# Routed rows of a mixture-of-experts layer: gathered through an index table built on chip, in place of a scatter into a slot buffer

## The reference

```python
def _L0_ffn_ref(x, router_w, w_fc, w_proj, shared_fc, shared_proj):
    TOP_K = 2
    flat = x.reshape(T, D)
    probs = softmax(flat @ router_w.T)               # 8 experts
    topk_p, topk_i = jax.lax.top_k(probs, TOP_K)
    topk_w = topk_p / jnp.maximum(topk_p.sum(-1, keepdims=True), 1e-09)
    combine = jnp.zeros((T, E)).at[jnp.arange(T)[:, None], topk_i].add(topk_w)
    for e in range(E):
        out = out + _mlp(flat, w_fc[e], w_proj[e]) * combine[:, e:e + 1]
    return out + _mlp(flat, shared_fc, shared_proj)  # _mlp: square(relu(x @ fc.T)) @ proj.T

x = x + 0.5 * _L0_ffn_ref(_layernorm(x), ...)
x = x + _L0_attn_ref(_layernorm(x), ...)             # a small MLP trained over 1024 steps, then applied
x = x + 0.5 * _L0_ffn_ref(_layernorm(x), ...)
```

## Time and profile before

| what | us |
|---|---|
| median of 3 runs | 660.36 (660.12 to 660.38) |
| profiled execution | 662.61, of which its span is 660.9 |
| MoE layer 0: tiles, first square to last matmul | 40.1 to 195.3 |
| middle layer, up to the second MoE layer's norm | 213 to 461 |
| MoE layer 1: tiles, first square to last matmul | 486.0 to 640.7 |

### The profile page before, as it was taken

The page is one execution under the profiler, slowest core; times in us unless marked ns, Lnnn a source line. Parts: engine busy times, 40 slices in busy tenths (PEclk is TensorE's granted clock), DMA queues, the critical chain, the costliest instruction groups (busy, mean ns, idle before and its releaser), DMA issues.

```text
span 660.9 us, 11626 instructions
## 1 busy us (share of the span) xinstructions
PE 499.5 (76%) x3496; PEld 445.3 (67%) x3496; DVE 331.5 (50%) x1204; ACT 297.8 (45%) x769; POOL 246.3 (37%) x365
## 2 busy tenths in 40 slices
PE   0673269999980789999999999955671279999970
PEld 0562169999970479999999999832561179989970
DVE  4751045344335557777777777726650035434423
ACT  3321035777760245555455455432420045767750
POOL 2047700444450123545445455430047600444440
PEclk9987569999995699999999999978566579999995
DMA  9921106000009500000000000000001160001007
GB/s 277 239 44 49 52 0 160 28 28 28 32 19 219 66 1 1 1 1 2 1 1 2 1 1 2 0 1 1 0 28 53 49 158 1 27 28 34 28 18 190
DMA packets 41146, 31.01 MB, mean 47 GB/s; under 512 B 3806, under 2 KB 36709, under 8 KB 41088
## 3 DMA queue, kind: packets, MB, share of 16 engines
q1 hardware_dynamic: 36544, 21.80, 14.3%
q0 software_dynamic: 4544, 8.47, 3.9%
HBM read 15.55 MB, written 15.61 MB: 47 GB/s over the span
## 4 chain that ended last, share of the span: by engine, by line
PE 65%; another core or an unknown queue 11%; DVE 10%; ACT 4%; DMA 3%; issue 3%; POOL 2%; SPq 1%; DVEq 0%; ACTq 0%; POOLq 0%
PE bank L916 18%; PE bank L567 14%; PE bank L557 7%; PE bank L550 4%; PE bank L548 4%; PE bank L549 4%; PE bank L504 2%; DMA stage<-y_dram 2%; PE bank L816 2%; DVE stats L379 1%; PE bank L837 1%; PE bank L818 1%; ACT sq L861 1%; PE bank L531 1%
## 5 line engine op out<-in xcount | busy, mean ns | idle before, releaser
L1029 POOL DMA_INDIRECT y_dram<-y_out,stage x78 | 75.8, 972 | 157.6 <-ACT y_out L646 145.6
L1236 DVE TENSOR_TENSOR sq<-bank,relu 128x512 f32<-128x512 f32 x110 | 75.9, 691 | 115.4 <-ACT relu L632 56.1
L567 PE MATMUL bank<-proj_w,hid_t 128*128 (+1 forms) x880 | 123.2, 286 | 11.0 <-issue 10.8
L567 PEld LDWEIGHTS bank<-proj_w,hid_t 128*128 128x128 f32 x880 | 113.3, 201 | 12.5 <-issue 12.5
L632 ACT ACTIVATE relu<-bank 128x512 f32<-128x512 f32 x110 | 65.8, 598 | 119.9 <-PE bank L550 60.8
L557 PE MATMUL bank<-ident,sq 128*128 128x128 f32 x440 | 70.4, 285 | 55.5 <-DVE sq L1236 41.8
L557 PEld LDWEIGHTS bank<-ident,sq 128*128 128x128 f32 x440 | 56.9, 147 | 75.1 <-DVE sq L1236 46.1
L1023 POOL DMA_INDIRECT slots_dram<-rows,slots x64 | 63.3, 989 | 99.6 <-issue 53.1
L638 ACT COPY hid_t<-bank 128x512 f32<-128x512 f32 x110 | 63.9, 581 | 27.2 <-remote 13.9
L911 POOL TENSOR_TENSOR sq<-sq,last_rows 128x128 f32<-128x128 f32 x48 | 22.0, 458 | 86.3 <-DVE sq L892 86.3
L1241 DVE SCALAR_TENSOR_TENSOR res<-bank,res 128x128 f32<-128x128 f32 x32 | 9.3, 291 | 66.5 <-remote 59.6
(11 more groups left out here) (238 smaller groups left out, 1285.1 us busy)
## 6 DMA issues: line engine op xcount, KB each, us to landing
slots_dram<-pad SPq DMA_DIRECT2D x2, 2535.0 KB, 20.2
stage<-slots_dram SPq DMA_DIRECT2D x18, 260.0 KB, 5.6
stage<-y_dram SPq DMA_DIRECT2D x16, 256.0 KB, 5.0
stage<-experts SPq DMA_DIRECT2D x3, 768.0 KB, 8.4
proj_w<-experts SPq DMA_DIRECT2D x1, 2304.0 KB, 15.9
y_dram<-y_out,stage POOLq DMA_INDIRECT x78
res<-x SPq DMA_DIRECT2D x2, 512.0 KB, 5.8
slots_dram<-rows,slots POOLq DMA_INDIRECT x64
```

The costliest lines, as they stand in the source:

```text
L567: last = nc.tensor.matmul(bank[4 + i % 2][:, 0:P], hid_t[:, i % 2, f_cols], proj_w[:, k, f_cols], start=j == 0, stop=j == FJ - 1)
L1029: nc.gpsimd.indirect_dma_start(y_dram.ap(), bass.IndirectOffsetOnAxis(tiles[:, t, P:P + 1].bitcast(U32), 0), y_out[:, t % YBUFS, :], None, ...
L1236: nc.vector.tensor_tensor(sq[:, i % 2, :], bank[i % 2][:], relu[:, i % 2, :], ALU.mult)\
```

## The change

- The scatter, the DRAM slot buffer, its fill and its reload are gone, and so are ACT's copy of `ln` and the 130-wide rows (`ln` is a tile of its own). SP stores `ln` to `ln_dram` once per layer.
- After L455 `route` splits each slot number into tile and row and makes `tile_id`: for each of the 32 (choice, block) columns, 40 numbers that hold the token's id + 1 in the column of its tile, else 0. VectorE makes `row_hot`, a 128-wide one-hot of the row, in four parts, one ahead of each of the turns 0 to 3 (`make_hot`). TensorE adds 32 products of the two in bank 7, eight behind each of the turns 1 to 4 (`table`): a 128 x 40 table with the id + 1 of the pair in each slot. In turn 5 VectorE turns it into two index lists, `to_row` and `from_row` (`make_index`).
- POOL then gathers each tile's 128 rows of 128 numbers from `ln_dram` by one indirect DMA: 20 tiles at once (GATHERED), then one more ahead of each of the waits for `y_made` of tiles 0 to 18. The y scatters stay, 39 per layer, with `to_row` as index.
- The limits of the index check lie in two registers set once.
- `y_out` has 8 buffers. ACT only copies into it; the weight is applied in `add_routed`, by one `scalar_tensor_tensor` for each block and choice (32 of 128 columns a layer, where there were 8 adds of 512).

```diff
-YBUFS = 4
+YBUFS = 8
...
             dve_link(dve, nc.vector.tensor_reduce(slot_f[:], where[:].rearrange("p k b e -> p (k b) e"), AX.X,
                                                   ALU.add), at)
-            nc.vector.tensor_copy(slots[:], slot_f[:]).then_inc(slots_done, 1)
+            dve_link(dve, nc.vector.tensor_copy(slots[:], slot_f[:]), at)
+            nc.vector.tensor_scalar(slot_row[:], slots[:], P - 1, None, ALU.bitwise_and)
+            dve_link(dve, nc.vector.tensor_scalar(slot_tile[:], slots[:], 7, None, ALU.logical_shift_right), at)
+            hot = [P, NSLOT, NCOL]
+            dve_link(dve, nc.vector.tensor_tensor(tile_id[:], iota_t[:].unsqueeze(1).to_broadcast(hot),
+                                                  slot_tile[:].unsqueeze(2).to_broadcast(hot), ALU.is_equal), at)
+            nc.vector.tensor_tensor(tile_id[:], tile_id[:].bitcast(F32), ids[:].unsqueeze(2).to_broadcast(hot),
+                                    ALU.mult)
...
+        def make_hot(c):
+            n = NSLOT // HOT
+            hot = [P, n, P]
+            c = slice(c * n, (c + 1) * n)
+            nc.vector.tensor_tensor(row_hot[:, c, :], iota_p[:].unsqueeze(1).to_broadcast(hot),
+                                    slot_row[:, c].unsqueeze(2).to_broadcast(hot), ALU.is_equal).then_inc(hot_done, 1)
+        def make_index(dve, at, f):
+            dve.wait_ge(table_done, f + 1)
+            table = bank[7][:, 0:NT]
+            dve_link(dve, nc.vector.tensor_scalar(empty[:], table, 0.0, float(NO_ROW), ALU.is_equal, ALU.mult), at)
+            dve_link(dve, nc.vector.scalar_tensor_tensor(to_row[:], table, -1.0, empty[:], ALU.add, ALU.add), at)
+            nc.vector.tensor_scalar(from_row[:], to_row[:], T - 1, None, ALU.bitwise_and).then_inc(index_done, 1)
...
+            def table(c):
+                pe.wait_ge(hot_done, f * HOT + c + 1)
+                for n in range(c * NSLOT // HOT, (c + 1) * NSLOT // HOT):
+                    last = nc.tensor.matmul(bank[7][:, 0:NCOL], row_hot[:, n, :], tile_id[:, n, :], start=n == 0,
+                                            stop=n == NSLOT - 1)
+                if c == HOT - 1:
+                    last.then_inc(table_done, 1)
...
-                nc.scalar.mul(y_out[:, t % YBUFS, :], bank[4 + i % 2][:, 0:P], tiles[:, t, P + 1:P + 2])\
-                  .then_inc(y_made, 1)
+                nc.scalar.copy(y_out[:, t % YBUFS, :], bank[4 + i % 2][:, 0:P]).then_inc(y_made, 1)
...
             def pool_tiles(f):
-                for b in range(NBLK):
-                    for k in range(TOPK):
-                        n = k * NBLK + b
-                        nc.gpsimd.indirect_dma_start(slots_dram[f].ap(),
-                                                     bass.IndirectOffsetOnAxis(slots[:, n:n + 1], 0),
-                                                     rows[:, k, b, :], None, bounds_check=NT * P - 1,
-                                                     oob_is_err=False).then_inc(scattered, 16)
+                def gather(t):
+                    if f == 0 and t == NT - 3:
+                        pool.wait_ge(w_lo_done, E + 1)
+                    nc.gpsimd.indirect_dma_start(tile_rows(t), None, ln_dram.ap(),
+                                                 bass.IndirectOffsetOnAxis(from_row[:, t:t + 1], 0),
+                                                 bounds_check=from_limit, oob_is_err=False)\
+                      .then_inc(tiles_in[t // GRP], 16)
+                pool.wait_ge(index_done, f + 1)
+                pool.wait_ge(ln_stored, 16 * (f + 1))
+                for t in range(GATHERED):
+                    gather(t)
                 for t in range(NT):
+                    if t + GATHERED < NT:
+                        gather(t + GATHERED)
                     pool.wait_ge(y_made, f * NTILES + NS + t + 1)
-                                                 bass.IndirectOffsetOnAxis(tiles[:, t, P:P + 1].bitcast(U32), 0),
-                                                 y_out[:, t % YBUFS, :], None, bounds_check=TOPK * T - 1,
+                    nc.gpsimd.indirect_dma_start(y_dram.ap(), bass.IndirectOffsetOnAxis(to_row[:, t:t + 1], 0),
+                                                 y_out[:, t % YBUFS, :], None, bounds_check=to_limit,
                                                  oob_is_err=False).then_inc(y_stored[t % YBUFS], 16)
...
                 for i in range(NTILES + 2):
+                    if i < HOT:
+                        make_hot(i)
+                    elif i == HOT + 1:
+                        make_index(dve, at, f)
                     if i < NTILES:
                         squared(i)
...
+                        for b in range(g * GRP, (g + 1) * GRP):
+                            last = nc.vector.scalar_tensor_tensor(
+                                res[:, b, :], y_rows[:, k, b * P:(b + 1) * P], weight[:, k, b:b + 1], res[:, b, :],
+                                ALU.mult, ALU.add)
```

More of the change, by code:

```diff
@@ L31 @@
 NTILES = NS + NT
+NCOL = NT + NT % 2
 NQ = (NT + GRP - 1) // GRP
-ROW = P + 2
-PAD_ROW = 1 << 20
+NSLOT = TOPK * NBLK
+NO_ROW = 1 << 13
+HOT = 4
+GATHERED = 20
 PER_WORD = 8
 NWORDS = (NT + PER_WORD - 1) // PER_WORD
-YBUFS = 4
+YBUFS = 8
 NLOADS = 3
@@ L143, in mk_macaron @@
         res = sb("res", [P, NBLK, P])
-        rows = sb("rows", [P, TOPK, NBLK, ROW])
-        ln = rows[:, 0, :, 0:P]
+        ln = sb("ln", [P, NBLK, P])
         ln_t = sb("ln_t", [P, T])
@@ L189, in mk_macaron @@
         where = sb("where", [P, TOPK, NBLK, E])
-        slot_f = sb("slot_f", [P, TOPK * NBLK])
-        slots = sb("slots", [P, TOPK * NBLK], U32)
+        weight = sb("weight", [P, TOPK, NBLK])
+        slot_f = sb("slot_f", [P, NSLOT])
+        slots, slot_row, slot_tile = (sb(n, [P, NSLOT], I32) for n in ("slots", "slot_row", "slot_tile"))
+        row_hot = sb("row_hot", [P, NSLOT, P], F32R)
+        tile_id = sb("tile_id", [P, NSLOT, NCOL], F32R)
+        empty = sb("empty", [P, NT])
+        to_row, from_row = (sb(n, [P, NT], U32) for n in ("to_row", "from_row"))
         n_tiles = sb("n_tiles", [P, E])
@@ L234, in mk_macaron @@
                                for n in range(3))
-        squares = y_out
-        slots_dram = [nc.dram_tensor(f"slots_dram{f}", (NT * P, ROW), F32) for f in range(2)]
+        squares = y_out[:, 0:4, :]
+        ln_dram = nc.dram_tensor("ln_dram", (T, P), F32)
         y_dram = nc.dram_tensor("y_dram", (TOPK * T, P), F32)
@@ L516, in tile_q, with tile_rows, tiles_in_group @@
             return (i - NS) // GRP
+        def tile_rows(t):
+            return stage[:, (E + 1) * 2 * F - (t + 1) * P:(E + 1) * 2 * F - t * P]
+        def tiles_in_group(q):
+            return min(GRP, NT - q * GRP)
         def tile_cols(i):
@@ L586, in pe_tiles @@
                     transposed(tile_q(i + 3))
+                if 1 <= i <= HOT:
+                    table(i - 1)
         def pe_out_rows(pe, g):
@@ L935, in _ @@
             load_params(sp, params_in)
[L937 to L939 removed]
             def sp_tiles(f):
[L942 to L948 removed]
+                sp.wait_ge(ln_done, (2 * f + 1) * NBLK)
+                sp.dma_start(ln_dram.ap().rearrange("(b p) d -> p b d", p=P), ln[:]).then_inc(ln_stored, 16)
                 for n in range(YBUFS):
@@ L1062, in _ @@
                     pool_key_part(pool, *key_part(4 * step.n + n))
-            nc.gpsimd.memset(squares[:], 0.0).then_inc(new_squared, 1)
+            nc.gpsimd.memset(squares, 0.0).then_inc(new_squared, 1)
             for turn in range(NBLK):
@@ L1309, in _ @@
             dve.wait_ge(gap_done, 2 * NBLK)
-            nc.vector.tensor_reduce(norms[:], squares[:], AX.X, ALU.add).then_inc(norms_done, 1)
+            nc.vector.tensor_reduce(norms[:], squares, AX.X, ALU.add).then_inc(norms_done, 1)
             dve.wait_ge(total_done, 1)
```

77 lines of the change are left out of this document (30 added, 47 removed).

## The result

| | before | after |
|---|---|---|
| median of four runs | 660.37 us (660.12 to 660.84) | 683.08 us (679.44 to 684.33) |
| ratio, 95% interval | | 1.034 (1.031 to 1.036) |
| profiled execution, its span | 662.61, 660.9 | 683.5, 681.7 |
| granted TensorE clock, mean | 0.877 | 0.89 |

A forecast was written before the change was run, and what follows sets the result against it. TensorE bounds the routed part, and packed indirect DMAs stall the shared part. Shorter stalls in both layers -20, add stages +3, sum -17 of 662.6; median 643.4, plus 2 for lag: 645 us, range 605 to 675.

The forecast's parts named there:

- second rival: Routed part, turns 18 to 36: packed indirect DMAs stall it, 8 to 20 us a layer more, 672 us; chance 0.27.
- Step 6: Routed part, turns 18 to 36: POOL lags 8.2 us behind TensorE, but y_out's eight buffers cover it, costing nothing.
- step 3: 32 table matmuls on TensorE: 4.2 to 7.6 us a layer, 2.5 on the path; index operations 0.5.
- Steps 1 and 7: Route tail before the first square: 4.8 us a layer; add stage with eight operations for two: 1.5 us a layer.
- step 4: Index there in turn 5, 57.5 us in layer 0; 20 gathers at 1.28 us fill POOL to 83; no wait.
- The burst's stall: Shared part: with 20 gathers the stall lasts from 65 to 87 in layer 0, 22 us in place of 38.
- The first rival: Shared part: scatters into DRAM cause the stall, so gathers bring none; 53 us gained, 608 us; chance 0.30.

The follow-up runs named there:

- x4: After with its gathers left out, SP loading the same bytes from block rows by plain DMAs: 615.11 us, where before took 660.2.
- all_gap_mid: After with a 256-column memset behind every indirect DMA: 638.36 us beside before at 657.72 (with stall); 627.96 beside 627.76 (without).
- all_gap_small: After with a 64-column memset behind every indirect DMA: 679.81 us beside before at 657.72 (with stall); 615.17 beside 628.3 (without).
- z_after_again: After, unchanged, run again in a batch without the stall: 615.15 us, beside 628.3 for before.
- z_before_again: Before, unchanged, run again in a batch without the stall: 625.27 us, beside 628.3 for before.
- x2: After with a 768-column memset and a wait behind each of the first 20 gathers of a layer: 668.06 us, where before took 660.2.
- x5: Before with an 8-column memset and a wait behind each of a layer's 32 scatters: 661.31 us, where before took 660.2.

## Why the prediction was wrong

The time fell outside the range, on the side of the second rival (660 to 684, given 0.27).

- **Step 6 failed: "the lag itself costs nothing".** It counted what POOL owes (two indirect DMAs a turn) against buffers, and held the pace of TensorE for given. At a pitch of 1.32 us TensorE's signals come late, y_out comes late, and each three turns carry a pause: 3.07 us a turn against the 2.13 of the forecast and the 2.8 to 3.2 that the rival named. It cost 16.8 and 15.2 us a layer, where the rival had 8 to 20. Shown, in batches with the stall: x4 takes the gathers away and 16.6 us are gone (79.1); all_gap_mid widens the pitch by 0.16 us against all_gap_small and the routed part is 6.2 us shorter, the shared part 14.3. Without the stall the same kernel at the same pitch keeps TensorE's pace (z_after_again, 79.1), as step 6 had it. So the step failed on the delay of the signals, not on its count of buffers. The reason that I gave against the rival, that a late y_made gives the pause by itself, is what the trace shows, but the pause is the cost.
- **The lesser miss: layer 1's shared part.** From first square to index there were to be 12.6 us; it took 14.1 in layer 0 and 17.2 in layer 1. The granted clock was 0.79 in that stretch of layer 0 and 0.64 in that of layer 1, and two of the four groups of table matmuls ran at the lower level in layer 1 (one in layer 0), at the upper end of step 3. Another 3.8 us lie behind the index: from the first gather to the first y_out it took 46.4 us in layer 0 and 50.2 in layer 1. The first and the third group in layer 1:

```profile
500.41 1.88 PE L568 MATMUL bank<-tile_id,row_hot 128*128 128x40 f32 x8
...
511.47 1.05 PE L568 MATMUL bank<-tile_id,row_hot 128*128 128x40 f32 x8
```

  Without the routed loss layer 1 would have ended 2.9 us earlier than before (4.5 less 7.3), not 9.4.
- **The sum closes.** Forecast -17 for the profiled execution; routed parts +32.0, layer 1 up to its first y_out +6.5, the other terms between -1.5 and +1 each: +20.8, as measured on the span.
- **What held.** Steps 1 and 7, here in rows of VectorE:

```profile
39.06 1.49 DVE L469 TENSOR_TENSOR tile_id<-iota_t,slot_tile 128x1280 fp32r<-128x1280 int32 x1
40.59 1.49 DVE L471 TENSOR_TENSOR tile_id<-tile_id,ids 128x1280 fp32r<-128x1280 f32 x1
43.45 1.21 DVE L489 TENSOR_TENSOR row_hot<-iota_p,slot_row 128x1024 fp32r<-128x1024 int32 x1
44.58 0.67 DVE L1277 TENSOR_TENSOR sq<-bank,relu 128x512 f32<-128x512 f32 x1
...
58.54 0.18 DVE L498 TENSOR_SCALAR from_row<-to_row 128x39 uint32<-128x39 uint32 x1
...
211.45 2.31 DVE L1308 SCALAR_TENSOR_TENSOR res<-stage,weight,res 128x128 f32<-128x128 f32 x8
```

  1.49 each for 1280 columns (1.5), 1.21 for 1024 (1.25), the first square 4.45 later (4.8), the index at 58.72 (57.5), the eight adds 2.31 (1.8 to 2.3). Gathers are 1.00 + 0.30 apart, so step 4 stands. The burst's stall was shortened nearly as said: turn 11 was forecast at 87, and the square of turn 11 was made at 81.58, of turn 12 at 90.16. That is in part luck, since the stall was forecast from 65 to 87 and ran from about 71 (TensorE's matmul that ended at 71.01 was heard at 73.80) to 89.5. With its routed part at 2.08 us a turn layer 0 would have ended at 184.5; the forecast was 185.
- **The first rival (no stall, 608 us)** had the wrong reason. It laid the stall to scatters into DRAM. A gather does it as well (after), but there are batches in which neither does, and there the kernel takes 613 to 615. That this lies near 608 is luck: the gain of 53 us that the rival counted was never there, since before takes 625 to 628 in those batches, and the change gains 10 to 15.
- **What the rows of before could not show.** Its 35 us of stall a layer were not 35 to be had: z_before_again, with no stall, still needs 58.4 us for the shared part, only 17.9 less than 76.3, since the rows come late. The change removes this second bound too, and that is what it gains when nothing is late: 10.4 us of shared part in layer 0 (58.4 to 48.0), less the 4.5 us of its longer route.

**Open.** What delays the signals, since the trace shows the waits and not what holds the signal, and whether the tracing has a part in it; and what switches it between batches. The x and v batches share a chip and differ in it. Whether a POOL queue that runs ahead is needed, and whether all gathers first would carry the stall, was not settled.

## What to carry to other kernels

Count the indirect DMAs of POOL by their pitch, in each stage: where they would run packed, at 1.3 us here, price the stage twice, once at TensorE's pace and once at POOL's pace plus late signals, even when buffers cover the lag. In this kernel 1.50 us took most of the loss away, and the next wider pitch tried, 1.87, all late signals. Moving such work out of a stall into a stage that an engine fills moves the stall too, where there is one. Ask of every stall what stands behind it, by an experiment that removes it (here 8 columns of memset and a wait): if the time stays, the next bound was already there. And run the kernel before beside each change, for the sign of a change can hang on a condition that neither program contains.

## What the runs showed of the hardware that was not expected

- In the batches with the stall, indirect DMAs of 128 rows on POOL at a pitch of 1.28 to 1.34 us went with waits for TensorE's signals of up to 17.8 us (before), 10.0 (after), 7.3 (x2) and 6.5 (all_gap_small); at 1.46 to 1.50 at most 2.4; at 1.87, 2.03 and 2.50 none. In the other batches the same pitches went with none.
- The condition comes and goes by the batch: before took 658 to 660 us or 625 to 628 (660.2 and 627.8 on one and the same chip), after 683 or 613 to 615, and within a batch it held for all the runs (13 of before in one, between 626.8 and 631.1).
- In the batches with the stall the traces lack semaphore events of POOL's indirect DMAs: 213 of 1024 are there in before, 811 in x5; in the others 1022 or more. x4 shows it where nobody is late: 1128 of the 1248 events of its y scatters, against 1246 in z_after_again.
- An indirect gather of 128 rows holds POOL 1.00 us, 0.03 more than the scatter of before, with the same gap of 0.30, though the limits of its index check lie in registers.
